# Two graph layers on one core: query and key weights folded with the map, and the q, k and v products of layer 1 moved into the next round

## The chip, the core and the metric

The kernel runs on one core of a Trainium2 chip. The core has a matrix engine (TensorE, PE in the rows), VectorE (DVE), ScalarE (ACT), GpSimd (POOL) and a queue that issues transfers (SyncE, SP). Each engine works through its own list of instructions in order; they meet only at semaphores. TensorE writes to eight PSUM banks of 128 x 512 fp32 numbers, and VectorE and ScalarE read them. The metric is the device time of one execution in microseconds.

## What is computed

64 graphs of 256 nodes with 512 features each, and a mask `adj` of 256 x 256 per graph. Two layers, each a residual around an attention on a normalised input:

```python
h = jnp.maximum(_layernorm(x, axis=-1), 0.0)
x = x + L0(h, adj)        # 4 heads of 64: softmax(mask(q k^T / 8)) v, then Wo and bias
h = jnp.maximum(_layernorm(x, axis=-1), 0.0)
x = x + L1(h, adj)        # 8 heads of 64

# L1
m = h @ map_w.T + map_b
n = per head of m: sem / max(norm(sem), 1e-8)
cos_adj = (n n^T, masked) > 0.1
q = m @ q_w.T + q_b;  k = m @ k_w.T + k_b
p = softmax(where(mask, -1e10, q k^T / 8)) * keep
adj_h = cos_adj * p
Ax = adj_h @ (h @ gcn_map_w.T + gcn_map_b)
out = relu((Ax @ gcn_W.T) / (adj_h.sum(-1) + 1))
```

## The kernel before

All is written for one core in one function, `gnn_two_layers`. A **round** handles one graph n: all of layer 0 and the linear part of layer 1 (steps with a plain name); beside them runs the attention of layer 1 of the graph before, a = n - 1 (steps with a pair number p = 0 to 3, a pair being two of the eight heads). `rounds` writes the body once for graph 0 alone, once in a loop over 62 rounds, once for the last graph, and once for the attention that is then left over.

Every engine has a hand-written list that sets the order of its steps: `TENSOR`, `SCALAR`, `VECTOR`, `POOL` (GpSimd) and `SYNC`. A step that is on several lists is the parts of one piece of work. The steps:

- `ht0a`, `ht0b`: transposes of `h`, the normalised and cut input, into `hT`; `qk0` to `qk3`, `v0`: q, k and v of layer 0; `s0` to `s3`: its scores, `exp0` to `exp3`, `sum0` to `sum3`: its softmax; `pt0` to `pt3`: transposes of the probabilities; `av`, `wo0`, `wo1`: values and output. `norm1`: the row scaling for layer 1, after row statistics and `rstd1` on GpSimd; `stats0`, `rstd0`, `norm0`: the same for the next graph's input.
- `ht1a`, `ht1b`: transposes of the second `h`; `m0` to `m3`: the map; `ss`, `pow`, `rt`, `bc0`, `bc1`: one over the norm of every head's row, multiplied into `m32`; `unit` 0 and 1: the result split into two parts in `nrm`.
- `q0` to `q3`, `k0` to `k3`, `vv0`, `vv1`: q, k and v of layer 1.
- `score` p, `exp_a/b` p, `cos` p, `turn_a/b` p (transposes into `uT`), `value` p (into `oT`), `back` p (transposes back, then `rel`, which GpSimd adds to `x_res`), `factor` p (three tiny VectorE operations).

Products are taken in three matmuls of fp32r numbers, high part with high, high with low, low with high (`PASSES`). So each product is copied out twice: ScalarE writes the high part, VectorE then takes the difference. For `m`, VectorE does two operations (lines 670 and 671): the fp32 number into `m32` and the low part into `qkm`, which `q` and `k` multiply.

Steps with a plain name on `TENSOR` use banks 4 to 7 in turn (`bank_of`), and a step waits in `empty` until the step four places before it has left its bank. The attention of layer 1 has banks 0 to 3 of its own. `score` p waits for `k` p and for both `uT` of the pair before; `turn` waits for VectorE's gating of `att`; `cos` for `unit` and for `rel` of the pair before.

In the first round, weights are loaded in ten pieces through four slots (`PIECES`, `SLOT`) and split into high and low part by ScalarE and VectorE. `fold` multiplies `gcn_map` with `gcn_W` in five steps, into `w_v` and `bias_v`. The transfers of a round are issued by `SYNC` in this order: the next `x`, the finished graph out, the move of `x_mid` to `x_res`, the next `adj`; each waits for what it needs, and the later ones wait behind it.

Of the kernel before, what the change touches and what calls it, by code (L numbers as in the profile page):

```python
# [23 lines left out]
def gnn_two_layers(nc, x, adj, wq, wk, wv, wo, bo, map_t, map_b, q_t, q_b, k_t, k_b, gcn_map, gcn_map_b, gcn_t, out):  # L24
# [3 lines left out]
    DH = 64  # L28
# [899 lines left out]
```

## Time and profile before

| | us |
|---|---|
| median of three runs | 4122.58 (4117.27 to 4124.95) |
| profiled execution | 4121.26 |
| its span | 4119.5 |
| busy: PE / PEld / DVE / ACT / POOL | 3931.4 / 3437.0 / 2608.3 / 1979.3 / 1324.3 |

PE is a matmul, PEld a weight load, which overlaps it. The page cuts the span into 40 slices and prints the busy share of each in tenths; TensorE stands at 9 in all but the first and the last, the granted clock of TensorE too (8 in these two), and VectorE at 6. A busy time says how full an engine is. What a wait costs is read from the order of time, where a number in square brackets is the engine's idle time ahead of a row and who ended it.

### The profile page before, as it was taken

What the parts mean: (1) busy time and instruction counts of PE and PEld (TensorE: products, weight loads), DVE (VectorE), ACT (ScalarE), POOL (GpSimd) and SP (SyncE); (2) the same over time, 40 slices, a digit from 0 to 9 for tenths busy, and PEclk for the clock granted to TensorE, in tenths of its full rate; (3) what the DMA queues carried; (4) which work ended last, traced back from release to release, by engine and by line L of the source; (5) the groups of instructions that cost most, each with busy time, mean ns of one, the idle gap of its engine ahead of it and who ended that gap; (6) DMA issues with size and microseconds to landing.
All of it is one profiled execution on the core that took longest, in us unless ns stands there. A gap on an engine that the chain in (4) does not pass through costs nothing.

```text
span 4119.5 us, 105002 instructions
## 1 busy us (share of the span) xinstructions
PE 3931.4 (95%) x32976; PEld 3437.0 (83%) x32976; DVE 2608.3 (63%) x9426; ACT 1979.3 (48%) x5583; POOL 1324.3 (32%) x2007
## 2 busy tenths in 40 slices
PE   7999999999999999999999999999999999999997
PEld 6888888888888888888888888888888888888886
DVE  4666666666666666666666666666666666666664
ACT  3554544544545445445454454454454544544544
POOL 3333333333332333333333333333333333333332
PEclk8999999999999999999999999999999999999998
DMA  3000000000000000000000000000000000000000
GB/s 87 16 32 26 22 32 16 32 32 16 32 27 21 32 18 30 32 16 32 29 18 32 22 25 32 16 32 32 16 32 27 21 32 16 32 32 16 32 27 17
DMA packets 65544, 111.77 MB, mean 27 GB/s; under 512 B 20880, under 2 KB 22448, under 8 KB 65520
## 3 DMA queue, kind: packets, MB, share of 16 engines
q1 hardware_dynamic: 64928, 110.12, 7.8%
q0 software_dynamic: 592, 1.35, 0.2%
q8 instruction: 13, 0.21, 0.0%
q14 instruction: 11, 0.09, 0.0%
HBM read 44.34 MB, written 33.55 MB: 19 GB/s over the span
## 4 chain that ended last, share of the span: by engine, by line
PE 65%; DVE 12%; issue 11%; ACT 6%; POOL 4%; DVEq 1%; DMA 1%; POOLq 0%; ACTq 0%; SPq 0%
PE bank L755 34%; PE bank L763 9%; PE bank L748 7%; PE bank L783 6%; PE bank L775 4%; ACT prob L501 3%; PE bank L883 3%; POOL prob L417 2%; DVE x_mid L663 2%; ACT att L475 2%; DVE prob L650 2%; DVE att L607 2%; DVE att L618 1%; POOL rstd L362 1%; DVE hT L640 1%
## 5 line engine op out<-in xcount | busy, mean ns | idle before, releaser
L475 ACT ACTIVATE att<-att,nmax 128x256 f32<-128x256 f32 x1024 | 509.7, 500 | 299.6 <-DVE nmax L607 299.6
L417 POOL TENSOR_SCALAR prob<-prob,rsum 128x256 f32<-128x256 f32 x512 | 241.1, 487 | 631.2 <-DVE rsum L657 628.2
L755 PE MATMUL bank<-hT,w_qkv 128*128 128x256 f32 x3072 | 414.9, 288 | 4.7 <-DVE hT L640 4.7
L755 PE MATMUL bank<-qkm,w_k 128*128 128x256 f32 x3072 | 416.6, 285 | 0.0
L755 PEld LDWEIGHTS bank<-hT,w_qkv 128*128 128x128 f32 x3072 | 376.9, 189 | 37.9 <-issue 24.2
L755 PE MATMUL bank<-hT,w_map 128*128 128x256 f32 x3072 | 396.7, 285 | 5.1 <-DVE hT L640 1.0
L618 DVE SCALAR_TENSOR_TENSOR att<-bank,att 128x256 f32<-128x256 f32 x1024 | 392.3, 420 | 4.0
L755 PE MATMUL bank<-qkm,w_q 128*128 128x256 f32 x3072 | 390.8, 283 | 0.0
L755 PEld LDWEIGHTS bank<-hT,w_map 128*128 128x128 f32 x3072 | 372.5, 189 | 18.4 <-DVE hT L640 17.3
L763 PE MATMUL bank<-w_v,hT 128*128 128x512 f32 x1536 | 385.3, 399 | 0.0
L755 PEld LDWEIGHTS bank<-qkm,w_k 128*128 128x128 f32 x3072 | 380.1, 188 | 5.0
L481 ACT ACTIVATE uT<-bank 128x512 f32<-128x512 f32 x512 | 292.2, 598 | 181.1 <-PE bank L748 169.5
L515 ACT ACTIVATE q<-bank,bias_q 128x256 fp32r<-128x256 f32 x256 | 121.0, 473 | 537.1 <-PE bank L755 535.2
L607 DVE CUSTOM_DVE_ANT_0 att<-bank,mask 128x256 f32<-128x256 f32 x1024 | 372.1, 420 | 7.3 <-PE bank L775 2.3
L755 PEld LDWEIGHTS bank<-qkm,w_q 128*128 128x128 f32 x3072 | 373.4, 189 | 0.1
L763 PEld LDWEIGHTS bank<-w_v,hT 128*128 128x128 f32 x1536 | 278.6, 188 | 82.6 <-issue 24.2
L783 PE MATMUL bank<-uT,v 128*64 128x256 f32 x2048 | 280.1, 395 | 49.4 <-ACT uT L481 49.4
L410 POOL TENSOR_TENSOR x_res<-x_res,rel 128x256 f32<-128x256 f32 x256 | 189.0, 738 | 420.4 <-DVE rel L634 420.4
L689 DVE SCALAR_TENSOR_TENSOR q<-bank,bias_q,q 128x256 fp32r<-128x256 f32 x256 | 117.1, 478 | 321.4 <-ACT q L515 321.4
L359 POOL TENSOR_SCALAR var_e<-mv 128x2 f32<-128x2 f32 x128 | 24.7, 193 | 913.9 <-DVE mv L540 913.9
L634 DVE SCALAR_TENSOR_TENSOR rel<-bank,fac 128x256 f32<-128x256 f32 x256 | 108.7, 424 | 314.6 <-PE bank L820 310.1
L515 ACT ACTIVATE k<-bank,bias_k 128x256 fp32r<-128x256 f32 x256 | 121.5, 474 | 373.9 <-PE bank L755 373.9
(122 smaller groups left out, 7949.6 us busy)
## 6 DMA issues: line engine op xcount, KB each, us to landing
x_in<-x SPq DMA_DIRECT2D x64, 512.0 KB, 3.4
x_res<-x_mid SPq DMA_DIRECT2D x64, 512.0 KB, 3.1
out<-x_res SPq DMA_DIRECT2D x64, 512.0 KB, 2.8
adj<-adj SPq DMA_DIRECT2D x64, 64.0 KB, 2.6
att<-gcn_map POOLq DMA_DIRECT2D x2, 512.0 KB, 9.0
x_mid<-wq SPq DMA_DIRECT2D x1, 512.0 KB, 5.6
x_res<-wk SPq DMA_DIRECT2D x1, 512.0 KB, 6.8
v<-wv SPq DMA_DIRECT2D x1, 512.0 KB, 7.7
```

The source lines that it names most:

```text
L410: g.tensor_tensor(part, part, rel[:, :, :], ALU.add).then_inc(res_added, 1)
L417: last = g.tensor_scalar(prob0[:, hd, c, :], prob0[:, hd, c, :], rsum0[:, hd, c:c + 1], 0.0, ALU.mult, ALU.add)
L475: s_.activation(e_sl, e_sl, ACT.Exp, bias=nmax1[:, p, c, e:e + 1], scale=-1.0, accum_out=esum1[:, p, c, e:e + 1]).then_inc(exp1_done, 1)
L481: s_.activation(uT[:, e, :], t_bank[e][:, :], ACT.Copy).then_inc(uT_ready, 1)
L515: s_.activation(dst[:, 0, t, :], bank[bank_of[kind]][:, 0:N], ACT.Identity, bias=bias[:, t:t + 1]).then_inc(high_done, 1)
L607: v_.tensor_tensor_reduce(out=att[:, p % 2, e, c, :], in0=score_bank[e][:, c * N:c * N + N], in1=mask1[:, c, :], scale=-SCALE, scalar=FLT_ ...
L618: v_.scalar_tensor_tensor(e_sl, gram_bank[e][:, c * N:c * N + N], COS_THRESHOLD, e_sl, ALU.is_gt, ALU.mult, accum_out=usum1[:, p, c, e:e + ...
L748: last = t_.transpose(dst[:, b * 128:b * 128 + 128], src_of(outer, c), ident[:, :])
L755: last = t_.matmul(dst, w(ws, k)[:, t * 128:t * 128 + 128], rhs[:, rs, k, :], start=(k == 0 and i == 0), stop=(k == KT - 1 and i == 2))
L763: last = t_.matmul(dst, lhs[:, ls, k, c * 128:c * 128 + 128], w(ws, k), start=(k == 0 and i == 0), stop=(k == chunks - 1 and i == 2))
L775: last[e] = t_.matmul(banks[e][:, c * N:c * N + N], left[r, ls, c * 128:c * 128 + 128], right[r, rs, :], start=(i == 0), stop=(i == 2))
L783: last = t_.matmul(dst[64 * e:64 * e + 64, :], v[:, jc, (hd0 + e) * DH:(hd0 + e + 1) * DH], rhs(e, jc), start=(jc == 0), stop=(jc == C - 1))
```

## The change

1. In the first round the query and the key weights are multiplied on the chip with the map: `w_q` becomes the product of map and query weight, and `bias_q` becomes query weight times map bias plus query bias; the same for the key. `fold` has 15 steps instead of 5: 0 to 3 and 4 as before, 5 and 10 for the two biases, 6 to 9 and 11 to 14 for the weights. The raw weights come in by four new transfers; `map_rows` is the map in its other orientation.
2. So q and k are taken from the second `h` and not from `m`. That `h` gets a buffer of its own, `gT`. `m` is written once, by ScalarE into `m32`, and VectorE has no part in it.
3. `q`, `k` and `vv` are now steps with a number, of graph a, in the round after: `("vv", 0)`, `("q", 0)`, ... They share banks 4 to 7 with the others, have semaphores of their own (`later_full`, `later_high`, `later_done`), and `q1` and `k1` hold two pairs instead of four.
4. All five lists but `SYNC` are written in another order. `POOL` begins with `mask0`.

The core of the diff:

```diff
     TENSOR = [
-        "ht0a", ("score", 0), "ht0b", ("cos", 0), "qk0", "qk1", ("turn_a", 0), "qk2", ("turn_b", 0), "s0", "s1", ("value", 0),
+        ("vv", 0), "ht0a", "ht0b", ("q", 0), "qk0", "qk1", "qk2", ("k", 0), "qk3", ("cos", 0), "s0", "s1", ("score", 0), "s2",
...
     POOL = [
-        ("unit", 0), "mid", "mask0", "sum0", "sum1", ("unit", 1), ("back", 0), "sum2", "sum3", "rstd1", ("back", 1),
-        ("back", 2), "m0", "rstd0", "m1", "m2", "m3", "pow", "mask1", ("back", 3)
+        "mask0", ("unit", 0), "sum0", ("unit", 1), "mid", "sum1", "sum2", "sum3", "rstd1", ("back", 0), "m0", "rstd0",
+        ("back", 1), "m1", "m2", "m3", "pow", ("back", 2), "mask1", ("back", 3)
     ]
...
-        PIECES += halves(map_t, w_map) + halves(q_t, w_q) + halves(k_t, w_k)
+        PIECES += halves(map_t, w_map)
...
+        BIAS_V, BIAS_Q, BIAS_K = 4, 5, 10
+        VALUE_W, QUERY_W, KEY_W = range(0, 4), range(6, 10), range(11, 15)
...
+        FOLD = {"s2": (0, 1), "pt0": (2, 3), "av": (4,), "ht1a": (5, 6), "m0": (7,), "m1": (8,), "m2": (9,),
+                first(TENSOR, TAIL + ("m3",)): (10, 11, 12, 13, 14)}
...
+                        if a is None:
+                            sp.wait_ge(fold_full, VALUE_W[-1] + 1)
+                            sp.sem_inc(passed_sync, 1)
+                            sp.dma_start(map_raw, by_rows(map_rows)).then_inc(map_raw_in, 16)
+                            for i, f in ((0, BIAS_V), (1, QUERY_W[-1])):
+                                sp.wait_ge(fold_full, f + 1)
+                                sp.sem_inc(passed_sync, 1)
+                                sp.dma_start(k_raw[i], by_rows(k_t)[:, 2 * i:2 * i + 2, :]).then_inc(k_raw_in, 16)
...
+                if f in (BIAS_Q, BIAS_K):
...
+                    for t in range(KT):
+                        for k in range(KT):
+                            last = t_.matmul(full[:, t:t + 1], raw(k)[:, t * 128:t * 128 + 128], bias_m[:, k:k + 1], start=(k == 0), stop=(k == KT - 1))
+                else:
+                    t = f - (QUERY_W if query else KEY_W)[0]
+                    for k in range(KT):
+                        last = t_.matmul(full[:, :], map_raw[:, k, t * 128:t * 128 + 128], raw(k), start=(k == 0), stop=(k == KT - 1))
...
-                        s_.activation(dst[:, 0, t, :], bank[bank_of[kind]][:, 0:N], ACT.Identity, bias=bias[:, t:t + 1]).then_inc(high_done, 1)
+                        s_.activation(m32[:, t, :], bank[bank_of[kind]][:, 0:N], ACT.Identity, bias=bias_m[:, t:t + 1]).then_inc(m_ready, 1)
...
-                    elif kind in ("m0", "m1", "m2", "m3"):
-                        t = int(kind[1])
-                        v_.tensor_scalar(m32[:, t, :], full[:, 0:N], bias_m[:, t:t + 1], None, ALU.add)
-                        v_.scalar_tensor_tensor(qkm[:, 1, t, :], full[:, 0:N], bias_m[:, t:t + 1], qkm[:, 0, t, :].bitcast(F32),
-                                                ALU.add, ALU.subtract).then_inc(product_done, 1)
...
+                    if kind in ("q", "k", "vv"):
+                        pe.wait_ge(product_done, out_of_psum(a, "ht1b"))
+                        empty(a, n, s)
+                        if kind == "vv":
+                            last = project_rows(full[:, :], gT, KT, p, lambda s2, k: w_v[:, s2, k, :])
                         else:
+                            w = {"q": w_q, "k": w_k}[kind]
+                            last = project(full[:, 0:N], lambda s2, k: w[:, s2, k, :], p, gT)
+                        last.then_inc(later_full, 1)
+                        continue
```

TensorE from `m3` to the end of a round, in the copy of the round that stands behind the loop; kernel before. `uT,v` is `value` 3, `w_v` `vv0` and `vv1`, `half_of` `ss`, `ident,oT` `back` 3, `ident,rn` `rt`, `rnT,pick` `bc0` and `bc1`:

```order
180 L755 MATMUL bank<-hT,w_map 128x256 x12
181 L783 MATMUL bank<-uT,v 64x256 x4
182 L763 MATMUL bank<-w_v,hT 128x512 x12
183 L883 MATMUL bank<-half_of,ptm 128x2 x8
184 L755 MATMUL bank<-qkm,w_q 128x256 x36
185 L755 MATMUL bank<-qkm,w_k 128x256 x12
186 L820 MATMUL bank<-ident,oT 128x128 x2
187 L889 MATMUL bank<-ident,rn 8x128 x2
```

The same place in the changed kernel, from `m3` and `value` 2 to `vv` 0 of the next round (`k,q` is `score` 3, `nrm` `cos` 3, `ident,att` `turn` 3):

```order
204 L909 MATMUL bank<-gT,w_map 128x256 x12
205 L937 MATMUL bank<-uT,v 64x256 x4
206 L929 MATMUL bank<-k,q 128x256 x12
207 L983 MATMUL bank<-ident,oT 128x128 x2
208 L1049 MATMUL bank<-half_of,ptm 128x2 x8
209 L929 MATMUL bank<-nrm 128x256 x12
210 L902 MATMUL bank<-ident,att 128x128 x8
211 L1055 MATMUL bank<-ident,rn 8x128 x2
212 L937 MATMUL bank<-uT,v 64x256 x4
213 L1061 MATMUL bank<-rnT,pick 128x256 x4
214 L983 MATMUL bank<-ident,oT 128x128 x2
215 L917 MATMUL bank<-w_v,gT 128x512 x12
```

The ten products of q, k and v have left this place, and all of pair 3 from its score on has come to it.

TensorE from `wo` to `ht1b`, same copy of the round, kernel before (`ident,h` is `ht1a` and `ht1b`, `k,q` `score` 3, `nrm` `cos` 3):

```order
171 L763 MATMUL bank<-w_o,oT 128x512 x12
172 L748 MATMUL bank<-ident,att 128x128 x8
173 L783 MATMUL bank<-uT,v 64x256 x4
174 L775 MATMUL bank<-k,q 128x256 x12
175 L820 MATMUL bank<-ident,oT 128x128 x2
176 L748 MATMUL bank<-ident,h 128x128 x8
177 L775 MATMUL bank<-nrm 128x256 x12
```

And in the changed kernel (`gT,w_k` is `k` 2 and, further down, `k` 3; `gT,w_q` is `q` 2 and `q` 3; `uT,v` `value` 1):

```order
189 L917 MATMUL bank<-w_o,oT 128x512 x12
190 L902 MATMUL bank<-ident,att 128x128 x4
191 L909 MATMUL bank<-gT,w_k 128x256 x12
192 L909 MATMUL bank<-gT,w_q 128x256 x12
193 L902 MATMUL bank<-ident,att 128x128 x4
194 L909 MATMUL bank<-gT,w_q 128x256 x12
195 L902 MATMUL bank<-ident,h 128x128 x4
196 L937 MATMUL bank<-uT,v 64x256 x4
197 L909 MATMUL bank<-gT,w_k 128x256 x12
198 L983 MATMUL bank<-ident,oT 128x128 x2
199 L902 MATMUL bank<-ident,h 128x128 x4
```

Three products and a turn stand between `wo` and the first transposes now, and a fourth product between the two transposes. On VectorE the piece that answers to it reads, in the changed kernel, from the statistics behind `wo` (`stats<-x_mid`) to the copies of `q` 2 and `k` 2:

```order
341 L625 BN_STATS stats<-x_mid 128x6
342 L632 BN_AGGR mv<-stats 128x2 x2
343 L733 SCALAR_TENSOR_TENSOR att,usum<-bank,att 128x256 x2
344 L638 TENSOR_SCALAR h<-x_mid,mv,rstd 128x512 x2
345 L697 SCALAR_TENSOR_TENSOR q<-bank,bias_q,q 128x256
346 L697 SCALAR_TENSOR_TENSOR k<-bank,bias_k,k 128x256
```

In this last copy of the round there is no next graph, so `stats0` is missing; in the loop it stands between the scaling of `h` and the copy of `q`.

## Rows read from the trace of the kernel before

**Rows 1.** The page: the span and each engine's busy time.
```profile
span 4119.5 us, 105002 instructions
PE 3931.4 (95%) x32976; PEld 3437.0 (83%) x32976; DVE 2608.3 (63%) x9426; ACT 1979.3 (48%) x5583; POOL 1324.3 (32%) x2007
```

**Rows 2.** Waits of TensorE: waiting for whom, us in total, times, longest.
```profile
PE bank L748 <- DVE h L546: 93.6, 64, 8.3
PE bank L783 <- ACT uT L481: 49.4, 67, 0.8
```

**Rows 3.** Timeline of TensorE, one round: start, us, what [idle before].
```profile
2054.33 0.97 PE L775 MATMUL bank<-k,q 64*128 64x256 f32 x12
...
2087.26 1.09 PE L748 MATMUL bank<-ident,h 128*128 128x128 f32 x8 [1.35 <-DVE h L546]
...
2097.08 3.07 PE L763 MATMUL bank<-w_v,hT 128*128 128x512 f32 x12
2099.99 1.84 PE L883 MATMUL bank<-half_of,ptm 128*128 128x2 f32 x16
2101.69 4.50 PE L755 MATMUL bank<-qkm,w_q 128*128 128x256 f32 x36
2106.03 1.58 PE L755 MATMUL bank<-qkm,w_k 128*128 128x256 f32 x12
...
2117.49 0.98 PE L775 MATMUL bank<-k,q 64*128 64x256 f32 x12
```

**Rows 4.** Timeline of TensorE: second round's `ht0a`, last graph's `score` 0.
```profile
96.12 0.60 PE L748 MATMUL bank<-ident,h 128*128 128x128 f32 x4
...
4077.93 0.98 PE L775 MATMUL bank<-k,q 64*128 64x256 f32 x12
```

**Rows 5.** Groups of VectorE by line: busy, mean ns, idle before.
```profile
L670 DVE TENSOR_SCALAR ptm<-bank,bias_m 128x256 f32<-128x256 f32 x256 | 122.7, 479 | 5.2 <-ACT qkm L515 4.4
```

**Rows 6.** Timeline of VectorE: scaling of `h`, then statistics of the next input.
```profile
2085.80 1.40 DVE L546 TENSOR_SCALAR h<-x_mid,mv,rstd 128x512 f32<-128x512 f32 x2 [1.32 <-POOL rstd L362]
...
2094.60 1.29 DVE L533 BATCH_NORM_STATS2 stats<-x_in 128x6 f32<-128x512 f32 x2
```

**Rows 7.** Timeline behind the last round, where one pair at a time runs.
```profile
4079.13 0.43 DVE L607 CUSTOM_DVE_ANT_0 att<-bank,mask 128x256 f32<-128x256 f32 x1 [0.40 <-PE bank L775]
...
4080.85 0.42 DVE L618 SCALAR_TENSOR_TENSOR att<-bank,att 128x256 f32<-128x256 f32 x1
...
4081.34 0.65 PE L748 MATMUL bank<-ident,att 128*128 128x128 f32 x4 [1.38 <-DVE att L618]
...
4085.25 0.44 PE L820 MATMUL bank<-ident,oT 128*128 128x128 f32 x2 [0.48 <-ACT oT L485]
...
4085.78 0.42 DVE L634 SCALAR_TENSOR_TENSOR rel<-bank,fac 128x256 f32<-128x256 f32 x1 [3.04 <-PE bank L820]
...
4089.89 0.66 PE L748 MATMUL bank<-ident,att 128*128 128x128 f32 x4 [0.20 <-DVE att L618]
...
4090.58 0.60 ACT L481 ACTIVATE uT<-bank 128x512 f32<-128x512 f32 x1 [0.26 <-PE bank L748]
4091.23 1.93 PE L783 MATMUL bank<-uT,v 128*64 128x256 f32 x8 [0.69 <-ACT uT L481]
```

**Rows 8.** Timeline: the norms' squares out of PSUM, then the power on GpSimd.
```profile
2038.70 0.17 DVE L692 TENSOR_SCALAR ssq<-bank 128x16 f32<-128x16 f32 x1 [3.97 <-PE bank L883]
...
2038.96 2.90 POOL L441 TENSOR_TENSOR rn<-ssq,minus_half 128x16 f32<-128x16 f32 x1 [2.88 <-DVE ssq L692]
```

**Rows 9.** Timeline of TensorE: a fold of the gcn weights, fp32.
```profile
46.24 2.26 PE L725 MATMUL bank<-gcn_w,att 64*128 64x64 f32 x16
```

**Rows 10.** Timeline of the transfer queue, and the page's transfers (KB, us to landing).
```profile
2048.52 0.40 SPq L310 DMA_DIRECT2D out<-x_res  x1
2051.41 0.47 SPq L321 DMA_DIRECT2D x_res<-x_mid  x1
2052.12 0.39 SPq L326 DMA_DIRECT2D adj<-adj  x1
...
x_in<-x SPq DMA_DIRECT2D x64, 512.0 KB, 3.4
...
adj<-adj SPq DMA_DIRECT2D x64, 64.0 KB, 2.6
```

More of the change, by code:

```diff
@@ L55, in gnn_two_layers @@
-        "m3", ("value", 3), "vv0", "ss", "q2", "q1", "q0", "k1", ("back", 3), "rt", "k0", "q3", "k3", "bc0", "bc1", "k2",
-        "vv1"
[4 rows of a table added]
+        ("turn_b", 2), "m3", ("value", 2), ("score", 3), ("back", 2), "ss", ("cos", 3), ("turn_a", 3), ("turn_b", 3), "rt",
+        ("value", 3), "bc0", "bc1", ("back", 3)
     ]
     SCALAR = [
-        ("unit", 0), "ht0a", "ht0b", ("exp_a", 0), ("exp_b", 0), "qk0", "qk1", ("turn_a", 0), ("unit", 1), "qk2",
-        ("turn_b", 0), "exp0", ("value", 0), "exp1", "qk3", ("exp_a", 1), ("exp_b", 1), "exp2", "exp3", "pt0", "pt1",
@@ L61, in gnn_two_layers @@
-        ("turn_a", 1), ("turn_b", 1), "pt2", "pt3", ("value", 1), "av", ("exp_a", 2), ("exp_b", 2), ("turn_a", 2),
-        ("turn_b", 2), ("value", 2), "ht1a", "ht1b", ("exp_a", 3), "m0", ("exp_b", 3), "m1", ("turn_a", 3), "m2",
-        ("turn_b", 3), "m3", "q2", ("value", 3), "q1", "k1", "q0", "k0", "q3", "k3", "k2"
+        ("unit", 0), "ht0a", "ht0b", ("unit", 1), ("q", 0), "qk0", "qk1", ("k", 0), "qk2", "qk3", "exp0", ("exp_a", 0), "exp1",
+        "exp2", "pt0", ("exp_b", 0), ("turn_a", 0), "exp3", ("k", 1), "pt1", ("turn_b", 0), "pt2", ("q", 1), "pt3",
@@ L64, in gnn_two_layers @@
+        ("value", 0), "av", ("exp_a", 1), ("exp_b", 1), ("turn_a", 1), ("turn_b", 1), ("q", 2), ("k", 2), ("q", 3),
+        ("value", 1), "ht1a", "ht1b", ("k", 3), ("exp_a", 2), "m0", ("exp_b", 2), "m1", ("turn_a", 2), "m2", ("turn_b", 2),
+        "m3", ("value", 2), ("exp_a", 3), ("exp_b", 3), ("turn_a", 3), ("turn_b", 3), ("value", 3)
     ]
     VECTOR = [
-        "ht0a", "ht0b", ("score_a", 0), ("score_b", 0), ("cos_a", 0), "qk0", ("cos_b", 0), "qk1", "s0", "qk2", "s1",
-        ("factor", 0), "sum0", ("back", 0), "sum1", "qk3", ("score_a", 1), ("score_b", 1), "s2", ("cos_a", 1), "s3",
@@ L711, in _ @@
             pe.sem_inc(o_full, PAIRS1)
-            def fold(kt):
-                if kt == 0:
-                    pe.wait_ge(pick_made, 3)
-                if kt == KT:
-                    pe.wait_ge(fold_done, KT)
-                for half in range(2):
-                    part = slice(64 * half, 64 * half + 64)
-                    for i in range(4):
-                        hd = 4 * half + i
-                        left = gcn_rows[part, i, kt * 128:kt * 128 + 128] if kt < KT else gcn_bb[part, i, :]
-                        last = t_.matmul(bank[kt % KT][:, hd * DH:hd * DH + DH], left, gcn_w[part, :], start=True, stop=True)
-                    if half == 0:
-                        last.then_inc(fold_half, 1)
-                        pe.wait_ge(fold_half, kt + 1)
-                last.then_inc(fold_full, 1)
@@ L886, in body @@
                         pe.wait_ge(rn_done, n + 1)
-                        empty(n, kind)
+                        empty(a, n, kind)
                         for c in range(C):
```

294 lines of the change are left out of this document (211 added, 83 removed), and 10 rows, old and new, of tables (TENSOR, VECTOR).

## The prediction, made before the changed kernel was run

> **What bounds the kernel now.** I read the page first: TensorE is busy 95% of the span and no other engine passes 63% [rows 1]. Then who TensorE waits for [rows 2]: 93.6 us in 64 waits for `h` and 49.4 us in 67 for `uT`; everything else is small. So only some 188 us of the span are not TensorE work. Then one round in order of time [rows 3]: the first score product of a round starts at 2054.33 and that of the next at 2117.49, a period of 63.16 us, of which 0.74 us (before `value` 2, the 49.4 us over 67 rounds) and 1.35 us (before `ht1a`) are waits. 61.07 us are left. Some 0.5 us of them are small waits that show only as a late weight load (before `pt3` and before `m0`), so the real work is about 60.5 us. The run is 96.1 us of start (to `ht0a` of the second round), 63 such periods with 2.2 us of extra, and 41.6 us after 4077.93, where the last graph's attention runs alone [rows 1, 4].
>
> Two things follow. A round can be shortened by at most some 2.6 us, only where TensorE waits. And each 0.1 us of wait per round costs 6.3 us of the total; 0.2% of the time, about what a measurement of this kernel can tell from no change, is 8.2 us, that is 0.13 us per round.
>
> **Work of a round.** The folding removes no matmul: q, k, v and map keep 12 matmuls for each of their 14 products. It removes eight VectorE operations per round (both forms of `m`, 0.48 us each [rows 5], of which some 0.08 lies beside the next), some 3.2 us. ScalarE keeps its four for `m`. VectorE is not the bound, so these 3.2 us count only where VectorE is the one waited for. Six products of 12 matmuls now stand in one run; in a run one costs 1.45 (36 in 4.34 us, from start to start [rows 3]), after another kind some hundredths more. I take 0.2 us for that: 60.35 us of work per round.
>
> **The wait for `h` (1.35 us) goes.** In the new order VectorE has the two sums of `wo`, four statistics, then `cos_b` 1, then `norm1`; TensorE has `turn_a` 1, `k` 2, `q` 2, `turn_b` 1, `q` 3 between `wo` and `ht1a`. Counted from the start S of `score` 1: `wo` starts at S+1.64, its first half reaches VectorE at S+3.34, sums and statistics end at S+6.5, and the 1.31 us to the row scaling over GpSimd, then 1.40 us of it [rows 6], make `h` ready at S+9.2. TensorE gets there at S+9.7. No wait, with 0.5 us to spare.
>
> **But a wait takes its place at `k` 3.** Its bank is that of `k` 2, and `k` 2 leaves it only when VectorE has done `norm1`, then `stats0` (1.29 [rows 6] and two aggregates, 1.6 us), then `q` 2 and `k` 2 (0.9): S+9.1+1.6+0.9 = S+11.6. TensorE arrives at S+11.2. That is 0.45 us.
>
> **The wait for `uT` (0.74 us) goes** inside the round, since `value` 0 to 2 now stand behind products. It comes back at the end. Count from V, the start of `value` 2. TensorE: `score` 3 at V+1.01, `back` 2 at +1.92, `ss` at +2.25 (1.70 long [rows 3]), `cos` 3 at +3.95. VectorE must first do `back` 2 (0.53 us after TensorE's start, so +2.45), then four score pieces at 0.345 (to +4.17), then `ss`; the cos product reaches it 1.20 us after its start, as a score product does [rows 7], at +5.15. From the second cos piece to the turn are 0.49 us [rows 7]: `turn_a` 3 at +5.99, where TensorE arrived at +4.86 (wait 1.13). `turn_b` 3 at +6.68 (0.26). `rt` needs `pow`, which starts 0.26 us after `ss` on VectorE and takes 2.90 [rows 8]: +7.39 (0.3). `value` 3 needs the second `uT`: 0.69 us from turn to copy and 0.65 from the copy's start to TensorE's [rows 7]: +8.02 (0.42). `bc0` at +9.03, and the next round's `vv` 0 writes the bank of `bc0`, so it waits for its copy (0.52 + 0.68 us): V+10.28 instead of +9.94 (0.34). Together 2.45 us. The tail of the kernel before is the witness for this: there the same chain, with nothing behind it, makes TensorE wait for `att`, `uT` and `oT` at each pair [rows 7].
>
> **Period:** 60.35 + 0.45 + 2.45 = 63.25 us against 63.16, so 63 rounds give +6 us. The sizes that I could not read are the transitions between kinds of matmul (0.2 us) and the 0.28 us from the last matmul of a product to its reader; together ±0.3 us a round, ±19 us.
>
> **Start.** The first round loses 17.4 us of q, k and v work (8 x 1.45 + 2 x 2.91) and the splitting of q_t and k_t, which delayed it. It gains two bias folds of 16 one-column matmuls (as `ss` with 16: 1.7 us each) and eight folds of four fp32 matmuls of 512 columns. No row shows such a matmul. Nearest from below are the fp32r matmuls with 512 columns at 0.243 us (12 of `w_v` in 2.91 [rows 3]); from above the fp32 folds of gcn, 16 matmuls of 64 columns in 2.26 us [rows 9], 2.20 to the next start, 0.1375 each, which scaled by columns gives 1.1 us. [...] By hand: `wo` ends at 53.3 (before 55.5), folds 5 and 6 to 58.5, `ht1` to 59.5, three times fold and `m` to 74.2, then 2.4 us of wait for the second half of k_t, whose transfer is issued only after fold 9, folds 10 to 14 to 92.2, `m3` 93.6, and `m3`, `ss`, `pow`, `rt`, `bc0` in a chain of 9.3 us: `vv` 0 of the second round at 103, against the 96.1 of `ht0a` [rows 4]. That is +7 us; by the lower end -13, by the upper +14.
>
> [...]
>
> **Tail.** Ahead of the last graph's `score` 0 now stand `vv` 0, `q` 0, `k` 0 and the copies of `k` 0: 7.1 us. The other 11.6 us of products stand in waits that were empty; by hand, pair by pair, 3.9 us of them show (`turn_b` 0 and `value` 0 come later). +11 us (7 to 14).
>
> **Sum:** 4119.5 + 6 + 7 + 11 = 4143.5 us of span; the profiled execution took 1.8 us more than its span and lies 1.3 us under the median of 4122.6. So **4145 us**, 0.55% slower.
>
> **Rivals.**
> *Faster: the end of the round hides more.* All of the round's old waits (2.6 us) go, and what is given back is one chain at one place, `score` 3 to `vv` 0. A lone pair in the tail has its turn 3.41 us after the score's start [rows 7]; I have 4.98, because `cos` 3 stands behind `ss`. If the cos pieces start 0.6 us sooner than I have them, the whole chain behind moves with them: 63 x 0.6 = 38 us, 4107 us. It decides from an end of 2.0 us of waits. For it: VectorE has 3.2 us less. Against it: VectorE's own row is not what is late there, TensorE's product is. 0.16.
> *Slower: the adjacency transfer.* GpSimd's list now begins with `mask0`, ahead of `unit` 0, for which `cos` 0 waits. `back` 3 on GpSimd ends 3.7 us after the round's start; then out is issued 0.24 later, the move 2.89 after that, adj 0.71 after that and lands in 2.6 [rows 10]; `mask0` 0.62 and `unit` 0 1.27 end at 12.1, and TensorE comes at 12.6. Landing in 3.4 us as x does [rows 10] would cost 0.3 us a round, +19: 4164 us. 0.16.
> [...]
> *The forecast,* 0.51, with a range of its own of 4125 to 4165; 0.07 of it within 0.2%, 0.01 faster.
>
> Faster 0.17, same 0.19 (0.07 + 0.12 of the cheap folds), slower 0.64. With the rivals' ends the range is 4106 to 4172.
>
> **What the next profile would show.** Right: no wait for `h` on TensorE in the loop; about 0.45 us before `k` 3; one cluster of five waits between `score` 3 and `vv` 0 of some 2.4 us, the longest for `att`; a period of 63.0 to 63.6; `w_v` of the second round first at about 103; the eight folds at 3.5 us each; some 52.6 us from the last `vv` 0 to the end. The forecast is wrong if the period is under 63.0 (then read the cluster), if TensorE waits for `nrm` at `cos` 0 (the transfer), or if the first `vv` 0 stands under 96 (the folds).

## The result: slower, and by more than predicted

| | before | after |
|---|---|---|
| median of three runs, us | 4122.58 (4117.27 to 4124.95) | 4189.45 (4189.41 to 4197.25) |
| profiled execution, its span | 4121.26, 4119.5 | 4197.25, 4195.4 |
| mean granted clock of TensorE, share of full | 0.993 | 0.961 |

After against before: 1.0169 with a 95% interval of 1.015 to 1.0189. The direction was right, the size was not: 4189 lies outside the range of 4106 to 4172. Two executions among the experiments below had a low granted clock and count in no time here: one of own_q0 (6349 us, clock 0.553) and one of own_q0_unit (4136 us, 0.917), from which that run's list of waits comes.

### The profile after

The page of the changed kernel, its first lines and the slices of TensorE and its granted clock; they answer to [rows 1]:

```profile
span 4195.4 us, 104525 instructions
PE 4026.8 (96%) x33104; PEld 3516.7 (84%) x33104; DVE 2467.8 (59%) x8920; ACT 2012.7 (48%) x5587; POOL 1320.7 (31%) x2007
...
PE   7999999999999999999999999999999999999998
...
PEclk8999999999999999999999999999999999999998
```

The slices show nothing but a digit: 9 where it was 9 before, and one slice is longer than a round. But TensorE is 95 us *busier* than before, although the folding adds, as forecast, only some 30 us of work and the rest is the same work. Its waits (waiting for whom, us in total, times, longest) answer to [rows 2]:

```profile
PE bank L902 <- DVE att L733: 67.3, 69, 1.7
PE bank L909 <- DVE k L697: 29.7, 62, 0.5
PE bank L937 <- ACT uT L570: 16.2, 65, 0.7
PE bank L917 <- DVE ptm L808: 15.7, 52, 0.4
PE bank L902 <- DVE h L638: 8.3, 1, 8.3
```

The wait for `h` has shrunk to one of 8.3 us at the start; `k` 3 waits 0.48 us in each of 62 rounds, and `turn_a` 3 0.96 us. The waits are smaller than before. What grew is the time that the same work takes. The timeline of TensorE at the end of a round follows (start, us, what, [idle before]); the first row is `value` 2, the last `vv` 0 of the next round. The trace prints each plain fp32 matmul as two records: `ss` is 8 matmuls in the program and x16 here, `value` is 4 and x8. An fp32r matmul or a transpose is one record (`score` 3: 12 and x12, `turn` 3: 8 and x8).

```profile
2023.00 1.08 PE L937 MATMUL bank<-uT,v 128*64 128x256 f32 x8
2024.02 0.98 PE L929 MATMUL bank<-k,q 64*128 64x256 f32 x12
2024.92 0.44 PE L983 MATMUL bank<-ident,oT 128*128 128x128 f32 x2
2025.20 1.85 PE L1049 MATMUL bank<-half_of,ptm 128*128 128x2 f32 x16
2026.97 1.34 PE L929 MATMUL bank<-nrm 64*128 64x256 f32 x12
2029.27 1.97 PE L902 MATMUL bank<-ident,att 128*128 128x128 f32 x8 [0.96 <-DVE att L733]
2031.03 0.64 PE L1055 MATMUL bank<-ident,rn 128*8 128x128 f32 x2
2031.93 1.97 PE L937 MATMUL bank<-uT,v 128*64 128x256 f32 x8 [0.26 <-ACT uT L570]
2033.83 0.91 PE L1061 MATMUL bank<-rnT,pick 128*128 128x256 f32 x4
...
2035.28 3.07 PE L917 MATMUL bank<-w_v,gT 128*128 128x512 f32 x12 [0.32 <-DVE ptm L808]
```

The four matmuls (eight records) of `value` take 1.08 us in the first row and 1.97 in the eighth. The stretches of this round say why (us, busy of PE, PEld, DVE, ACT, POOL, then PEclk, the granted clock, and two numbers for the transfers):

```profile
2023.00:2026.97 3.97, 3.97 (x39) 3.29 (x38) 1.51 (x8) 1.58 (x5) 0.61 (x1) 1.00 0.00 0
2026.97:2029.27 2.30, 1.34 (x13) 1.04 (x13) 1.20 (x8) 1.36 (x6) 1.85 (x1) 0.59 0.00 0
2029.27:2035.28 6.01, 5.43 (x25) 3.48 (x25) 2.21 (x8) 1.60 (x4) 1.75 (x2) 0.59 0.00 0
```

Behind `ss` and through the waits the granted clock falls to half of full for some microseconds: it is 0.50 from 2028.00 to 2033.83. It falls so in most rounds and at differing places: from one `ss` to the next there are ten periods of 62.5 us, 29 of 63.4 to 63.7 and 24 of 64.3 and more. In the kernel before, all 61 between the first and the last are 63.1 or 63.2.

### The profile page after: what moved, and what is told of

Same layout as the page of the kernel before. It is cut to its first block, busy times and chain, and to the rows that moved or that the text cites. A ratio compares the mean times of both kernels' runs of the same rounds, so it can differ in the third digit from the quotient of the medians.

```text
span 4195.4 us, 104525 instructions
## 1 busy us (share of the span) xinstructions
PE 4026.8 (96%) x33104; PEld 3516.7 (84%) x33104; DVE 2467.8 (59%) x8920; ACT 2012.7 (48%) x5587; POOL 1320.7 (31%) x2007
## 3 DMA queue, kind: packets, MB, share of 16 engines
q0 software_dynamic: 592, 1.35, 0.2%
## 4 chain that ended last, share of the span: by engine, by line
PE 84%; DVE 6%; issue 5%; POOL 1%; ACT 1%; DVEq 1%; DMA 1%; POOLq 0%; SPq 0%; ACTq 0%
PE bank L909 29%; PE bank L917 18%; PE bank L929 13%; PE bank L902 10%; PE bank L937 8%; PE bank L1049 2%; PE bank L983 2%; DVE stats L625 1%; POOL rstd L426 1%; DVE x_mid L779 1%; PE bank L1061 1%; ACT uT L570 1%; DVE mv L632 1%; DVE ptm L808 1%; DVE h L638 1%
## 5 line engine op out<-in xcount | busy, mean ns | idle before, releaser
L909 PE MATMUL bank<-gT,w_k 128*128 128x256 f32 x3072 | 422.7, 287 | 31.0 <-DVE k L697 29.7
L909 PEld LDWEIGHTS bank<-gT,w_k 128*128 128x128 f32 x3072 | 379.9, 189 | 60.1 <-DVE k L697 57.9
L909 PE MATMUL bank<-gT,w_q 128*128 128x256 f32 x3072 | 421.4, 286 | 0.0
L917 PE MATMUL bank<-w_v,gT 128*128 128x512 f32 x1536 | 395.3, 406 | 15.9 <-DVE ptm L808 15.7
L909 PE MATMUL bank<-gT,w_map 128*128 128x256 f32 x3072 | 397.7, 285 | 0.0
L902 PE MATMUL bank<-ident,att 128*128 128x128 f32 x2048 | 331.8, 299 | 67.9 <-DVE att L733 67.3
L909 PEld LDWEIGHTS bank<-gT,w_map 128*128 128x128 f32 x3072 | 371.9, 188 | 10.3 <-issue 1.9
L909 PEld LDWEIGHTS bank<-gT,w_q 128*128 128x128 f32 x3072 | 380.4, 189 | 0.1
L917 PEld LDWEIGHTS bank<-w_v,gT 128*128 128x128 f32 x1536 | 280.8, 190 | 99.1 <-DVE ptm L808 32.2
L902 PEld LDWEIGHTS bank<-ident,att 128*128 128x128 f32 x2048 | 262.6, 153 | 108.1 <-DVE att L733 90.4
```

Of the source, the lines that this page charges most:

```text
L902: last = t_.transpose(dst[:, b * 128:b * 128 + 128], src_of(outer, c), ident[:, :])
L909: last = t_.matmul(dst, w(ws, k)[:, t * 128:t * 128 + 128], rhs[:, rs, k, :], start=(k == 0 and i == 0), stop=(k == KT - 1 and i == 2))
L917: last = t_.matmul(dst, lhs[:, ls, k, c * 128:c * 128 + 128], w(ws, k), start=(k == 0 and i == 0), stop=(k == chunks - 1 and i == 2))
```

## The experiments

Theory at the start: the new order put the light work of `ss` and the one wait of 0.96 us close together, TensorE loses its clock there, and 63 rounds lose some 1.3 us each, 80 us. Rivals: the wait alone does it; the light matmuls alone do it; or the chain of waits is the loss and the clock only its sign. The kernel before, run beside them, had medians of 4120.7 to 4123.7 us.

### Filling the wait (fill4), and filling ss (fill4_ss)

```diff
+                    if s == ("turn_a", 3) and n is not None:
+                        empty(a, n, "rt")
+                        for _ in range(4):
+                            t_.matmul(bank[bank_of["rt"]][:, :], w_map[:, 0, 0, 0:128], w_map[:, 0, 0, :], start=True, stop=True)
```

> Edit: in the changed kernel TensorE gets four more fp32r matmuls of 512 columns (0.243 us each by the w_v row, 0.97 us together) right ahead of turn_a 3, where it waits 0.96 us for att; their result is never read. The profile of the changed kernel repeats a cycle of six rounds with periods of 62.5 to 64.6 us (mean 63.7), and the long ones have transposes, value 3 and bc0 at twice their length, at a granted clock of 0.5. Theory 1, the wait brings the clock down: filled with dense work, the clock stays at 1.00 through the round's end, every round takes about 62.5 us, 121 + 63 x 62.5 + 55 = 4114 us of span, some 4116 us in all, so 75 us less for MORE work. Theory 2, the light two-column matmuls of ss (1.84 us) bring it down: a filled wait changes nothing, 4185 to 4200 us, the six periods as before. Theory 3, the loss is the chain of waits and the clock is only a sign of it: the filler takes what the wait took, 4189 to 4200 us.

**4146.58 us** (4141.48 to 4147.41), clock 0.983: 43 us less than the changed kernel for 60 us more work. The list of waits has only 6.4 us for `att` left. 38 periods are 62.5 or 62.6 us, 23 are 63.8. So the chain theory falls, and the wait is one cause, not all of it.

> Edit: the changed kernel with four matmuls of 496 columns, one ahead of each quarter of ss, so that the light stretch holds dense work, while the wait of 0.96 us ahead of turn_a 3 stays empty. They delay ss, cos 3 and all behind by about 0.95 us, 60 us over 63 rounds. Theory 1, the wait alone brings the clock down: 4189 + 60 = 4250 us, half clock in the transposes of most rounds as before. Theory 2, the light columns of ss bring it down: the clock stays at 1.00 and 75 us come back, about 4175 us. If both count (how much TensorE does over the whole stretch), something between, also near 4175 to 4215.

**4199.82 us** in one run, clock 0.982. Between "wait alone" (4250) and "light work alone" (4175): 35 periods are at the clean 63.4, 26 at 64.4 to 64.6. Both count.

### Both at once (fill_both)

> Edit: both fillings of fill4 and fill4_ss in one kernel, four unread matmuls of 512 columns ahead of turn_a 3 and four of 496 inside ss. The first left half clock in about 24 of 62 rounds (periods 62.5 clean, 63.8 else), the second in 27 (63.5 clean with its 0.95 us of added work, 64.6 else). Theory, what counts is how much TensorE does over the whole of the round's end, waits and light work together: with both filled no round falls, every period is 63.5, 62 x (63.47 - 63.01) = 28 us over fill4, about 4175 us, granted clock 0.99. Rival, some other event of the round brings the clock down and the fillings only shift it: a third of the rounds still fall, about 4205 us.

**4174.36 us** in one run, against 4175 expected. All 61 periods inside the loop are the clean one, 63.4, at a clock of 0.993. Taking off the 0.95 us that the filling of `ss` costs in each round leaves 4114 us. By this estimate that is what the changed kernel would take with its clock held, 75 us less than it does and 8 us less than the kernel before.

### Light work alone, in the kernel before (before_ss2)

```diff
-                        for t in range(KT):
+                        for t in [*range(KT), *range(KT)]:
```

> Edit: the kernel before with the 16 two-column matmuls of ss done twice (same result), 1.7 us more of light work in each of 64 rounds, with no wait of TensorE near it. Theory 1, only a wait brings the clock down: granted clock 1.00 around ss, 4122 + 64 x 1.7 = 4231 us (up to 4240). Theory 2, light columns bring it down: 3.4 us of them are longer than the 1.84 of the changed kernel, the clock falls to 0.5 behind ss in most rounds and the products there take twice as long: 1 to 3 us more a round, 4300 to 4420 us.

**4296.74 us** in one run, a little under the 4300 of the second theory: its clean period is 64.9 us, 1.77 more than before, 113 us over 64 rounds, and 62 us come on top of them. 30 periods are 64.9 or 65.0, 28 are 66.4 or 66.5. In a long one the granted clock stands so, the second row being the products right behind `ss`:

```profile
2193.60:2198.00 4.40, 4.40 (x41) 4.36 (x40) 0.64 (x2) 0.00 (x0) 0.39 (x1) 1.00 0.00 0
2198.00:2203.00 5.00, 5.00 (x32) 5.00 (x31) 1.02 (x3) 1.22 (x3) 3.70 (x6) 0.66 0.00 0
```

TensorE is busy without a gap in both rows and falls all the same. 3.4 us of two-column matmuls (16 of them; the expectation counts their 32 records) do it in half of the rounds with no wait near; the 1.7 us of the kernel before, between `w_v` and `w_q` products, do not [rows 3]. The waits of the kernel before did not either, though together they are twice the 0.96 us: 0.74 us ahead of `value` 2 [rows 2] and, behind `value`, `score` 3 and two transposes, the 1.35 us for `h` [rows 3]. This is the stretch with the second of them, in the kernel before:

```profile
2085.85:2088.30 2.45, 1.10 (x11) 0.88 (x10) 2.19 (x6) 0.35 (x1) 0.69 (x2) 1.00 0.00 0
```

What the falls at a round's end have in common is a stretch in which TensorE computes little, by light matmuls, waits or both. How little is enough these runs do not say.

### Real work in the wait (own_q0), and the transfer (own_q0_unit, unit_first)

```diff
-"ss", ("cos", 3), ("turn_a", 3), ("turn_b", 3), "rt",
+"ss", ("cos", 3), "q0", ("turn_a", 3), ("turn_b", 3), "rt",
```

and `("q", 0)` is taken out of the start of the next round, on all three engines.

> Edit: the changed kernel with the one product q 0 taken back to the end of its own round, between cos 3 and turn_a 3 on TensorE, where the wait of 0.96 us is; its two copies stand on ScalarE ahead of turn_a 3 and on VectorE behind cos_b 3. Clock theory: real work of 1.45 us fills the wait and the clock holds at 1.00. turn_a 3 comes 0.35 us later, but rt still waits for pow, and vv 0 of the next round no longer waits for the bank of bc0 (0.32 us), so value 2 to vv 0 stays near 10.1 us and the next stretch is shorter by 1.45: period 22.43 + 10.1 + 28.4 = 60.9 us, 121 + 63 x 60.9 + 55 = 4013, about 4015 us in all, 2.6% under the kernel before. Chain theory (what q 0 leaves at the start of the round opens a wait there, for hT ahead of qk0, and the clock is a side effect): period 62.4 to 63.7, 4108 to 4189 us.

**4138 to 4155 us** in three executions, 1.0067 of before (1.0046 to 1.0087). The clock behaved (0.986), the sum did not: 4015 was expected. The waits of TensorE in this kernel begin with

```profile
PE bank L929 <- POOL nrm L466: 72.2, 62, 1.2
PE bank L909 <- DVE k L697: 29.7, 62, 0.5
PE bank L937 <- ACT uT L570: 28.2, 65, 0.7
```

and GpSimd shows where the first comes from:

```profile
2022.26 0.62 POOL L452 TENSOR_SCALAR mask<-adj 128x512 f32<-128x512 uint8 x1 [6.86 <-DMA adj<-adj]
2022.84 1.26 POOL L466 TENSOR_TENSOR nrm<-ptm,nrm 128x512 fp32r<-128x512 f32 x1
```

This is the prediction's rival of the adjacency transfer. With `q` 0 gone from the start of the round, `cos` 0 comes 1.5 us earlier and meets it.

```diff
-"mask0", ("unit", 0), "sum0",
+("unit", 0), "mask0", "sum0",
```

> Edit: own_q0 (q 0 in its own round between cos 3 and turn_a 3) with unit 0 ahead of mask0 in GpSimd's list. In own_q0 cos 0 waits 1.16 us in each of 62 rounds for nrm: GpSimd waits 6.86 us for the adjacency, does mask0 (0.62) and only then unit 0 (1.26), for which nothing is missing from 2012.6 on in the round read. Theory, the transfer is the cause: the clean period of 62.55 falls to 61.4, 4138 to 4155 become 4066 to 4083 us, and s 0 does not wait, since mask0 still ends at 2022.9 and the first s 0 product is there at 2024.7. Rival, something else is late as well (the copies of hT ahead of qk0, unit 0 itself behind back 3 on GpSimd): 0.5 us or less is gained, 4110 to 4140 us. If the clock still falls in a quarter of the rounds it costs 16 x 1.5 = 24 us, within both.

**4048.7 us** (four executions, 4045.9 to 4051.51), 0.9817 of before (0.98 to 0.9833). The wait for `nrm` is gone from the list. That is 17 us under the expected 4066.

> Edit: the changed kernel with unit 0 ahead of mask0 in GpSimd's list, alone. In the changed kernel GpSimd waits there for the adjacency in every round, but TensorE never waits for nrm: 4186 to 4194 us, periods as before between 62.5 and 64.6. Rival, the transfer also delays TensorE in the changed kernel in a way that shows only as a late weight load: up to 0.3 us a round less, 4170 us.

**4188.09 us** in one run: in the changed kernel itself the transfer costs nothing, as forecast with the larger chance.

### The wait before k 3 (stats_late) and the bias folds (bias_mix)

```diff
-"norm1", "stats0", ("q", 2), ("k", 2),
+"norm1", ("q", 2), ("k", 2), "stats0",
```

> Edit: the changed kernel with stats0 behind q 2 and k 2 in VectorE's list, so that the bank of k 2 comes free 1.6 us sooner. The wait of 0.48 us ahead of k 3 (29.7 us over 62 rounds) goes; VectorE's copies of ht1a come 1.6 us later, still ahead of m0. As a sum of waits: 4189 - 30 = 4159 us. With the clock: the clean period falls from 62.5 to 62.0, but how many rounds fall into half clock, and how deep, can change, as it did between 0 and 2.1 us from round to round of the changed kernel: anything from 4084 (no half clock in any) to 4190 us, 4159 if the mean loss of 1.2 us stays.

**4165.79 us**, 24 us less: the wait is gone from the list, its 30 us not quite, since the clock (0.96) cost a little more.

```diff
-                    for t in range(KT):
-                        for k in range(KT):
-                            last = t_.matmul(full[:, t:t + 1], raw(k)[:, t * 128:t * 128 + 128], bias_m[:, k:k + 1], start=(k == 0), stop=(k == KT - 1))
...
+                for k in range(KT):
+                    for j in range(KT if with_bias else 0):
+                        last = t_.matmul(bias_bank[:, k:k + 1], raw(j)[:, k * 128:k * 128 + 128], bias_m[:, j:j + 1], start=(j == 0), stop=(j == KT - 1))
...
                     last = t_.matmul(full[:, :], map_raw[:, k, t * 128:t * 128 + 128], raw(k), start=(k == 0), stop=(k == KT - 1))
```

> Edit: the changed kernel with the 16 one-column matmuls of each bias fold set in fours ahead of the four matmuls of the weight fold that follows, in place of one run of 16 ahead of it; same work. [...]

In the changed kernel the two bias folds, runs of 16 one-column matmuls, take 4.71 and 5.72 us at a granted clock of 0.73 and 0.60, and the weight folds behind them 5.64 and 6.35 us at 0.62 and 0.55. The theory was that the clock holds where the light matmuls stand between dense ones. Some 12 us were to go, so that `vv` 0 of the second round starts at 109 in place of 120.9. That was an estimate of mine, with 3.43 us for a weight fold (99.48 to 102.91 in the changed kernel) and 1.8 us for a bias fold, taken from the 1.84 us of `ss` [rows 3]; no run shows the 1.8.

**4188.61 us** in one run, and `vv` 0 starts at 118.29, not at 109. The query's folds gained: bias and first weight fold take 7.0 us (58.20 to 65.20, at a clock of 1.00) in place of 10.35. The key's took 12.3 in place of 12.1. They stand right behind the wait of 2.3 us for `k_t` and fell to half clock mixed or not (0.57 here). So half of the theory is confirmed, and 2.6 us of the 12 came. As for the 1.8 us: the 7.0 us less a weight fold of 3.43 leave 3.6 for a bias fold at full clock.

### Putting it together (best1, best1_fill2)

> Edit: the changed kernel with all of these: q 0 in its own round ahead of turn_a 3, unit 0 ahead of mask0, stats0 behind k 2, the bias folds mixed. Clean period 62.55 - 1.16 - 0.48 = 60.9 us; 109 + 63 x 60.9 + 55 = 4001 us with the clock at full in all rounds, some 4025 us with half clock in a quarter of them as in own_q0, 4075 us if in most. Rival, as the waits in the middle of the round go, others open that they hid (VectorE's queue, the row statistics, copies of hT): a clean period of 61.5 to 62, 4065 to 4100 us.

**4045.4 us** (4044.47 to 4048.89), 0.9807 of before (0.979 to 0.9823). The clean period is 60.8, reckoned 60.9; 27 of 63 are 62.2 or 62.3. In one of these the fall sits ahead of the waits, in `cos` 3 and `q` 0 (a granted clock of 0.60 and 0.55):

```profile
2079.91 1.85 PE L1053 MATMUL bank<-half_of,ptm 128*128 128x2 f32 x16
2081.68 1.44 PE L933 MATMUL bank<-nrm 64*128 64x256 f32 x12
2083.05 2.72 PE L913 MATMUL bank<-gT,w_q 128*128 128x256 f32 x12
2085.61 1.04 PE L906 MATMUL bank<-ident,att 128*128 128x128 f32 x8
```

> Edit: best1 with two unread matmuls of 512 columns (0.49 us) ahead of value 3, where TensorE waits 0.45 us for uT. best1 has 34 rounds of 60.8 and 27 of 62.3 us. Theory of the clock: with this wait filled too the rounds of 62.3 go, 27 x 1.5 = 40 us less and some 4 us more for the filling: about 4008 us; half of the rounds: 4028 us. Rival, two matmuls are too few against the light work of ss, or the rounds are of another origin: 4045 to 4050 us.

**4044.9 us**: no change, as its rival had it (4045 to 4050); the clock's theory was wrong by the full 37 us. 26 periods are still 62.2 or 62.3. In the round shown above the fall comes right behind `ss`, so a wait filled some microseconds later comes too late for it.

### The same work, spread (spread, spread_fill4)

The two matmuls (four records) of each quarter of `ss` are issued as soon as their squares exist:

```diff
-"m3", ("value", 2), ("score", 3), ("back", 2), "ss",
+"sa", "m3", "sb", ("value", 2), "sc", ("score", 3), ("back", 2), "ss",
```

> Edit: the changed kernel with the 16 two-column matmuls of ss no longer in one run: the four of each quarter stand where their squares are ready, ahead of m 3, ahead of value 2, ahead of score 3, and the last four behind back 2. Same work, one order changed on TensorE alone, the wait of 0.96 us for att ahead of turn_a 3 left in place. Clock theory: the light work no longer lies in the stretch of the wait. Were it all of the loss, all rounds were 62.5 us and the total about 4115 us; as the wait alone (fill4_ss) still gave half clock in 27 of 62 rounds at 1.1 us, about 4140 us. Rival, half clock needs no light run and the loss stays: 4185 to 4195 us. score 3 comes 1.3 us later on TensorE than counted from value 2 before, which may cost 0.1 to 0.3 us a round of new wait for att or uT (6 to 19 us), within both.

**4249.17 us** (4246.52 to 4252.52): 60 us *slower* than the changed kernel, 109 us over the expectation.

> Edit: spread with the four unread matmuls of fill4 in the wait ahead of turn_a 3. If the light run and the wait together are all of the loss, every round is clean: period 62.5 to 62.8, total 4114 to 4133 us at a granted clock near 0.99. If something else at the round's end (the single waits for uT and the bank of bc0, the transposes) also counts, a part of the rounds still falls: 4140 to 4170 us.

**4178.68 us** in one run at a clock of 0.994, 61 of 63 periods at 63.6. Two things follow. The clock: the filling, 60 us of added work, makes `spread` 70 us faster, with the granted clock at 0.994 in place of 0.967. The wait, not only `ss`, brings it down. And spreading opened waits, which the list of spread_fill4 shows:

```profile
PE bank L1066 <- POOL rn L506: 58.4, 64, 3.3
PE bank L910 <- DVE k L698: 29.8, 62, 0.5
PE bank L930 <- DVE rel L750: 21.0, 64, 0.7
```

`score` 3 is later on TensorE, VectorE reads `ss` only behind its four pieces, and so `pow` starts late (58.4 us in all). `cos` 3 comes so soon behind `back` 2 that its bank is not yet read (21.0).

### Spread, with the waits mended (best2, best2b, best3a, best3)

> Edit: best1 (q 0 in its own round, unit 0 ahead of mask0, stats0 behind k 2, bias folds mixed) with ss spread as in spread. best1 has 27 rounds at 62.3 against 60.8, with the fall right behind ss. Clock theory: all rounds 60.8, 4045 - 27 x 1.5 = 4005 us, to 4021 us where the later score 3 costs up to 0.25 us of wait for uT a round. Rival, the rounds fall all the same: 4045 to 4065 us.

**4057.79 us**, 0.9842 of before (0.9826 to 0.9859). Clock 0.992 and 61 periods of 61.6: not one round falls any more. But the two new waits eat it (56.6 and 21.0 us).

> Edit: best2 with the third quarter of ss behind score 3 in place of ahead of it, so that score 3 comes 0.45 us sooner, and eight of the light matmuls stand together with back 2 between them. If the later score 3 costs a wait in best2, this one is up to 0.25 us a round shorter (15 us less than best2); if the light matmuls together bring the clock down, some rounds of +1.5 us come back (5 to 40 us more). With neither, the same as best2 within 5 us.

**4050.47 us**: 7 us less than best2, from 61.6 to 61.5 a round; the wait for `pow` stayed (56.8 us), and the clock did too.

best3a moves VectorE's `ss` ahead of `score_a` 3. best3 takes the third quarter behind `back` 2, as room for that bank, and VectorE's `ss` between the two halves of the score:

```diff
-"sc", ("score", 3), ("back", 2), "ss",
+("score", 3), ("back", 2), "sc", "ss",
...
-("score_a", 3), ("score_b", 3), "ss",
+("score_a", 3), "ss", ("score_b", 3),
```

> Edit: best2 with VectorE reading ss ahead of score_a 3 in place of behind score_b 3, so that pow starts 1.3 us sooner. In best2 rt waits 0.87 us for pow at 89.42 in the round read, while value 3 behind it needs the second uT, which is there at about 89.3: so only some 0.45 us of it comes back, the rest turns into a wait for uT. Period 61.6 - 0.45 = 61.15, 4057 - 28 = 4029 us. Rival, the whole wait comes back: 4003 us. Other rival, the three added waits for the score pieces on VectorE (0.1 us) and a round's end that falls to half clock again: 4045 us or more.

**4038.74 us**, 0.9798 (0.9781 to 0.9814), 61.3 a round. The wait for `pow` is gone, and 30.9 us for `uT` stand in its place.

> Edit: best2 with the third quarter of ss behind back 2, together with the fourth, so that cos 3 no longer waits 0.32 us for back 2 to leave its bank, and VectorE reading ss between score_a 3 and score_b 3. Both waits go: 61.6 - 0.45 - 0.32 = 60.8 us a round, 4057 - 50 = 4008 us with the clock at full. Rival, eight light matmuls together with the transposes of back 2 ahead of them bring the clock down in some rounds at 1.5 us each (in best1 16 together did in 27 of 62): 4010 to 4050 us. Rival, pow still comes late by 0.3 us: 4025 us.

**3997.31 us** (3995.99 to 3999.63), 0.9699 of before (0.9682 to 0.9715), all 61 periods of the loop 60.6 or 60.7. The end of a round, to be read against the one of the changed kernel above:

```profile
2051.44 0.98 PE L934 MATMUL bank<-k,q 64*128 64x256 f32 x12
2052.35 0.44 PE L995 MATMUL bank<-ident,oT 128*128 128x128 f32 x2
2052.62 0.51 PE L972 MATMUL bank<-half_of,ptm 128*128 128x2 f32 x4
2052.99 0.59 PE L1060 MATMUL bank<-half_of,ptm 128*128 128x2 f32 x4
2053.51 0.98 PE L934 MATMUL bank<-nrm 64*128 64x256 f32 x12
2054.41 1.69 PE L914 MATMUL bank<-gT,w_q 128*128 128x256 f32 x12
2055.93 1.04 PE L907 MATMUL bank<-ident,att 128*128 128x128 f32 x8
2057.12 0.38 PE L1066 MATMUL bank<-ident,rn 128*8 128x128 f32 x2
2057.71 1.08 PE L942 MATMUL bank<-uT,v 128*64 128x256 f32 x8 [0.21 <-ACT uT L571]
...
2060.02 3.06 PE L922 MATMUL bank<-w_v,gT 128*128 128x512 f32 x12 [0.30 <-DVE ptm L809]
```

No row is at half clock (the granted clock from 2051.44 to 2063.00 is 1.00), and of the five waits between `score` 3 and `vv` 0 only 0.21 and 0.30 are left. So the folding with this order takes 3% off the kernel before, and the change as it was made gave that away. No run tells how much of the 3% is the folding: the kernel before was not tried in a better order.

## Why the prediction was wrong, step by step

The forecast span of 4143.5 us is, but for 1 us of rounding, 103 us of start, 63 periods with 2.2 us of extra, and 52.6 us of end. The profile has 120.93 us to the first `vv` 0, 4019.0 us to the last (4139.97), and 55.4 us behind it:

| step | forecast | measured |
|---|---|---|
| start | 103 | 120.9 (+18; see below) |
| 63 periods | 63.25 each | 63.79 each (+32 with the loop's 2 us of extra) |
| of that, half clock | none | some +80 |
| of that, the clean period | 63.25 | 62.5 (-0.75 each, -47) |
| end | 52.6 | 55.4 (+3) |

- **No wait for h:** right.
- **0.45 us before k 3:** right, 0.48 us. Its removal (stats_late) gave 24 us.
- **The chain at the round's end:** right as a chain. It was to be 10.28 us from `value` 2 to `vv` 0 at full clock. In the round that ends fastest `ss` comes 2.20 us behind `value` 2 and `vv` 0 8.05 behind `ss`: 10.25. The wait for `att` was sized 1.13 and is 0.96.
- **The missing step: the clock.** The prediction priced every matmul of the chain at full speed and its cluster of waits as waits alone. In the round shown above, the same chain takes 12.28 us; over the 63 rounds half clock costs some 80 us, which is more than the whole 44 us by which the forecast missed. The witness had been in [rows 7], in the very rows I used: the eight records of `value` at 1.93 us behind a lone pair in the tail, at a granted clock of 0.52. In the loop of the same kernel they take 1.08, at 1.00:

```profile
2083.55 1.08 PE L783 MATMUL bank<-uT,v 128*64 128x256 f32 x8 [0.74 <-ACT uT L481]
```

  I took the waits from [rows 7] and not the duration. None of my rivals had the clock, so the range had no room for it.
- **The work of a round, 60.35 us:** too high by some 0.7. Of the period of 63.25 us, the 10.28 from `value` 2 to `vv` 0 leave 52.97 for the rest. Measured are 29.86 from `vv` 0 to `score` 1 (2035.28 to 2065.14) and 22.42 from `score` 1 to `value` 2 (2000.58 to 2023.00), together 52.28. Between `vv` 0 and `score` 1 score products that follow one another come at 0.72 us, and transposes stand behind products. That this error, 43 us over 63 rounds, runs against the one of the clock is luck: with the work priced right the forecast would have been further off. This part is read from the timeline, not tried.
- **The start:** the fold of 3.5 us was right at full clock, but not by its working. No run shows the 0.87 us a matmul that it was added up from, an estimate of mine between the rows of `w_v` [rows 3] and of the gcn fold [rows 9]; the runs showed 0.86. The timeline of the second half of the key's folds has

```profile
92.28 0.99 PE L854 MATMUL bank<-bias_m,x_res 128*128 128x1 f32 x4
93.13 3.76 PE L858 MATMUL bank<-v,att 128*128 128x512 f32 x4
96.68 2.96 PE L858 MATMUL bank<-x_res,att 128*128 128x512 f32 x4
99.48 1.88 PE L858 MATMUL bank<-v,att 128*128 128x512 f32 x4
101.20 1.88 PE L858 MATMUL bank<-x_res,att 128*128 128x512 f32 x4
102.91 1.88 PE L858 MATMUL bank<-v,att 128*128 128x512 f32 x4
```

  Two rows are one fold, 3.43 us from start to start at full clock (99.48 to 102.91), so 0.86 us for an fp32 matmul of 512 columns (two records); forecast 0.87. The forecast took the 16 records of the gcn fold [rows 9] for 16 matmuls; the program has 8, so one of 64 columns costs 0.275 us and not 0.1375, and scaled by columns that gives 2.2 us, more than twice what came. That the 0.87 was right is luck. The first fold shown, for the most part at half clock, took 6.35.

  The same count failed openly in the bias folds. They were to take 1.7 us each, as `ss` with 16; but `ss` has 8 matmuls in its 1.7 us, a bias fold 16. At full clock that is 3.6 us (bias_mix); they took 4.71 and 5.72. That is 7.0 us over the forecast: 3.7 by the count, 3.3 by the clock. The two folds behind them took 5.64 and 6.35, 5.1 us more than 3.43 each, by the clock (0.62 and 0.55 of full). `wo` ended 5.8 us later than worked out; in the stretch from 27.8 to 42.0, ahead of it, the granted clock is 0.50, but what share of the 5.8 that makes was not separated. From the start of `m3` to `vv` 0 it took 11.6 in place of 10.8 (92.2 to 103). These are 18.7 us for the 18 missed; 8.4 of them are half clock in and behind the bias folds, and bias_mix gave 2.6 back.
- **The rivals:** the faster one, a shorter end, did not occur: the chain has its forecast length (10.25 us) where the clock holds. The adjacency transfer cost nothing here, and 1.16 us a round as soon as `cos` 0 moved forward (own_q0): the rival was the right one for the next kernel. The cheap folds, 0.12 in the chances: refuted by the 3.43 us a fold. At the 0.243 us of an fp32r matmul of 512 columns [rows 3], the lower end of the start, a fold would take 0.97.
- **The end:** 55.4 against 52.6. Its last 10.4 us are at a granted clock of 0.50, its stretch from 4170 to 4185 at 0.87; which of it makes the 2.8 us I did not separate. The last 9.5 us of the kernel before are at 0.50 too.

What stays open: why one round of the changed kernel falls to half clock in `cos` 3, the next only from `turn` 3 on, and one in six not at all. The sequence of periods repeats every six rounds (62.5, 63.5, 64.5, 64.5, 63.6, 63.5). It may depend on where the light stretch falls in time, but no run here was made to tell.

## What to carry to other kernels

Moving dense products away from a chain of waits and light matmuls can change the price of everything left there, as it did here (12.28 us at a granted clock of 0.72 for a chain that takes 10.25 where the clock holds): look for stretches in which TensorE would issue little, and price them at half clock as well. If they must exist, cut them up and fill the wait too: a few light matmuls at a time between products, and one product held back for the longest wait. Cutting up alone made this kernel 60 us slower (spread); with the product held back no round fell (best2). After each such move read the list of waits again, since it was a bank, a queue order or a transfer that took part of the gain back in several of the kernels here.

## What the runs showed of the hardware

- The granted clock fell to half of full although TensorE's busy share was near 1: 5.00 us busy of 5.00 at a clock of 0.66, of them 2199.00 to 2202.00 at 0.50, behind 16 two-column matmuls in 3.4 us (before_ss2). A busy TensorE is not a TensorE that computes much. In the changed kernel no wait at the end of a round of the loop is longer than 0.96 us.
- Unread dense work paid for itself here: four matmuls of 512 columns, 0.97 us a round, made the changed kernel 43 us (fill4) and `spread` 70 us faster (spread_fill4).
- A plain fp32 matmul is two records in the trace (`ss`: 8 in the program, x16). One of two columns costs 0.21 us at full clock (`ss`: 8 in 1.70 us), one of one column 0.43 at half (the last bias row above: 0.85 us for two), and one of 512 columns 0.86 us at full clock (99.48 to 102.91: 3.43 us for four), where an fp32r one costs 0.243 (12 in 2.91 us [rows 3]). Whoever prices from rows has to divide by the matmuls of the program, not by the records.
